# A mixture-of-experts layer on one Trainium2 core: from tile 32 on the shift rows stand eight tiles behind the rows in SyncE's list, and the padding stores go between later tiles

## The chip, the cores and the metric

The kernel runs on one core of one Trainium2 chip. Its time is the device time of one execution in microseconds; the time before is the median of three runs. Engines are named as the profile names them: PE is TensorE (matrix products, with PEld its weight loads), DVE is VectorE, ACT is ScalarE, POOL is GpSimd, SP is SyncE. SP computes nothing here: it works down a list of waits and DMA issues.

## The reference, cut to what matters

The input x is 16 sequences of 512 tokens with 128 features. A scan layer comes first; then every token goes to the best two of eight experts, each a pair of matrix products with a normalisation behind each.

```python
h = _layernorm(x, axis=-1) * (1 + ca) + sa
x = x + ga * _L0_attn_ref(h, ...)
h = _layernorm(x, axis=-1) * (1 + cb) + sb
x = x + gb * _L0_ffn_ref(h, ...)
...
def _L0_ffn_ref(x, Wr, br, W1, b1, g1, be1, W2, b2, g2, be2):
    logits = xt @ Wr + br
    p = jax.nn.softmax(logits, axis=-1)
    probs, idx = jax.lax.top_k(p, K)
    ...
    h = jnp.einsum('td,edf->etf', xt, W1) + b1[:, None, :]
    h = _layernorm(jax.nn.relu(h), g1, be1)
    y = jnp.einsum('etf,efd->etd', h, W2) + b2[:, None, :]
    y = _layernorm(jax.nn.relu(y), g2, be2)
    gate = (jax.nn.one_hot(idx, E, dtype=x.dtype) * probs[..., None]).sum(axis=1)
    out = jnp.einsum('te,etd->td', gate, y)
```

## The kernel before, in words

**Two phases.** In the first (`mixer_step`, to about 160 us) the 16 sequences pass the scan layer; the second normalisation gives rows h, and each token's row is written twice, once for each of its experts, into the DRAM tensor `expert_rows`, which has one region for each expert. POOL does that with indirect DMAs (`store_rows`, L703). In the second phase (`expert_step`, 160 to about 475 us) 135 tiles of 128 rows are worked off in order, tile i with the weights of one expert. A table in on-chip memory says for each tile from which row it starts and which expert it has.

**One tile.** The number behind each engine is the step in which it works on tile i; step s is the one in which PE computes the hidden layer of tile s.
- SP loads the tile's 128 rows into one of eight buffers `hrow` (`load_rows`, L549).
- PE turns them (`turn_rows`, L1650, step i-2), ACT and DVE split them into a high and a low part (L820, L1224).
- PE computes the hidden layer (L1667 to L1669, step i), ACT takes the relu (L824), DVE the statistics (L1229), PE turns it (L1675, step i+2), ACT copies it back (L828).
- PE multiplies it with the second weights (`values`, L1685, step i+4).
- DVE scales and shifts that product (v0, L1452, step i+5). For this it needs the first third of the tile's *shift row*: three vectors of 128 numbers of the expert, the same for all 128 partitions, which SP loads with one DMA of 192 KB (`load_shifts`, L570).
- ACT relu (L948), DVE statistics and vg (L1463, second third of the shift row, step i+7). The last third is added to give the result y: either by DVE itself (`direct`, L1444, odd tiles below 44 and the last five) or by ACT (L956) and POOL (`add_shift`, L719).
- DVE works out in step i, from the rows, where each result row goes (target, L1435); POOL stores y with an indirect DMA into `expert_results` (`store_results`, L731).

PE's four-tile beat: before every fourth tile PE also puts the first biases of four tiles into its banks (`biases`, L1659), so every fourth tile is longer.

**What sets SP's order.** SP's list is written out by hand. For each tile index i, `load_next(i)` (L571) issues: on every fourth i the table entries and the biases of four tiles (L528, L535, L561); then, after waiting until tile i-8 has been turned (`t3_done`) and its targets are computed (`target_ready`), the rows of tile i; then the shift row of tile i-6 (`SHIFT_LAG` is `SLOTS - 2`, 6). The shift row's buffer is free when the result y of the tile that used it last is done, so `load_shifts(j)` waits for that y. Buffers are shared as `ring` says: up to tile 31 there are sixteen, from tile 32 on eight. So the shift row of tile 40 is the first that waits for a tile only eight before it: for the y of tile 32.

```python
user = last_user(i)
if user is not None and direct(user):
    sp.wait_ge(direct_y_ready, direct_count(user))
elif user is not None:
    sp.wait_ge(y_ready, shifted_count(user))
```

**What else SP issues between tiles.** `store_padding(e)` (L596) writes 128 rows of padding behind the last row of expert e's region, one store for each of eight experts; on e = 0 and e = 4 it first loads four counts (L593). It must be done before the rows of tile 73 are loaded. `load_gb` (L627) comes after tiles 30, 32, 34 and 36. `load_early(b)` (L616, 512 KB) loads results of batch b for the output, after tile index 54 for b = 0, 61 for b = 1 and so on to 131; for b = 0 it waits in `results_of` (L609) until the results of tiles 31 to 38 have landed in DRAM. `store_early(b)` (L620) stores finished output.

Of the kernel before, what the change touches and what calls it, by code (L numbers as in the profile page):

```python
# [6 lines left out]
def adaln_ssm_moe_kernel(nc, x_in, win_in, bin_in, bp_in, cp_in, dp_in, wout_in, bout_in, wr_in, br_in,  # L7
# [27 lines left out]
    DI, NS = bp_in.shape  # L35
    CI = DI // P
    E, _, F = w1_in.shape
    CF = F // P
    TOPK = 2
# [3 lines left out]
    EXPERT_TILES = TOPK * NT + E - 1  # L43
# [9 lines left out]
    ROUND1 = (ROUND1_BATCHES * J * TOPK * P - E * (P - 1)) // P  # L53
# [14 lines left out]
    with ExitStack() as ctx:  # L68
# [13 lines left out]
        SLOTS = 8  # L82
# [166 lines left out]
        def direct(i):  # L249
            return i >= LAST_SHIFTED or i % 2 == 1 and i < ROWS_UNTIL  # L250

        def direct_count(i):
            return sum(direct(n) for n in range(i + 1))

        def shifted_count(i):
            return i + 1 - direct_count(i)
# [5 lines left out]
        def piece_tile(b, j):  # L262

            return FIRST_COMBINED + (b * J + j) * (LAST_PIECE - FIRST_COMBINED) // (EARLY * J - 1)
# [14 lines left out]
        def ring(i):  # L279

            return i % (2 * SLOTS) if i < WIDE_UNTIL else i % SLOTS
# [5 lines left out]
        def shift_lane(i):  # L287

            return ring(i) // 2 if i < WIDE_UNTIL else ring(i)
# [6 lines left out]
        def last_user(i):  # L296

            return max((m for m in range(i) if ring(m) == ring(i)), default=None)
# [148 lines left out]
        def tiles(b):  # L447

            return bass.ds(b * J, J)
# [3 lines left out]
        def _(sp):  # L453
# [72 lines left out]
            def load_row_numbers(i):  # L526
                ids = range(i, min(i + AT_ONCE, EXPERT_TILES))
                _, values = nc.values_load_multi_w_load_instructions(  # L528
                    tile_row[0:1, i:ids[-1] + 1], engines=(mybir.EngineType.SP,), min_val=0, max_val=SPARE + (NSPARE - 1) * P,
                    skip_runtime_bounds_check_because="cut off at the first and the last row where the table is written")  # L530
                row_of.update(zip(ids, values))
# [10 lines left out]
            def rows_of_batches(count):  # L542
                for m in range(ROW_LANES):
                    sp.wait_ge(rows_stored[m], row_groups(count, m))
# [3 lines left out]
            def load_rows(i, n):  # L548
                sp.dma_start(hrow[n], rows_d[bass.ds(row_of[i], P), :]).then_inc(hrow_loaded[n], 16)  # L549

            SHIFT_LAG = SLOTS - 2

            def load_b1(i):
                load_expert_numbers(i)
                if i == 0:
                    sp.wait_ge(b1_stored, 32)
                if i >= 2 * TOGETHER:
                    sp.wait_ge(h_done, i - 2 * TOGETHER + 1)
                for n in together(i):
                    part, turn = b1_rows(n)  # L560
                    sp.dma_start(b1_ring[part, turn, :].bitcast(F32), b1_d[bass.ds(expert_of[n], 1), :, :].rearrange("o k f -> (o k) f")  # L561
                                 ).then_inc(b1_loaded[turn], 16)

            def load_shifts(i):
# [5 lines that stand above are left out]
                sp.dma_start(shift_rows[ring(i)], shifts_d[bass.ds(expert_of[i], 1), :].broadcast_to([P, 3 * D])).then_inc(shifts_loaded[shift_lane(i)], 16)  # L570

            def load_next(i):
                if i % AT_ONCE == 0:
                    load_row_numbers(i)
                    load_b1(i)
                sp.wait_ge(t3_done, i + 1 - SLOTS)
                sp.wait_ge(target_ready, i + 1 - SLOTS)
                load_rows(i, i % SLOTS)
                load_shifts(i - SHIFT_LAG)

            for n in range(SLOTS):
                load_rows(n, n)
            for n in range(0, SLOTS, TOGETHER):
                load_b1(n)
            for n in range(SLOTS - SHIFT_LAG):
                load_shifts(n)
            count_of = {}

            def store_padding(e):
                if e == 0:  # L590
                    sp.wait_ge(counts_ready, 1)
                if e % AT_ONCE == 0:
                    _, values = nc.values_load_multi_w_load_instructions(  # L593
                        cnt_i[0:1, GROUPS - 1, e:e + AT_ONCE], engines=(mybir.EngineType.SP,), min_val=0, max_val=T)
                    count_of.update(zip(range(e, e + AT_ONCE), values))
                sp.dma_start(rows_d[bass.ds(count_of[e] + e * REGION, P), :], padding[:]).then_inc(padding_stored, 16)  # L596

            PADDED_AT = ROUND1 - E
            for i in range(SLOTS, ROUND1):
                load_next(i)  # L600
                if i >= PADDED_AT:
                    store_padding(i - PADDED_AT)
            FIRST_BATCHES = GROUP_ENDS[2]
            LAST_ROWS = FIRST_BATCHES * J * TOPK - E + 1
            sp.wait_ge(table_ready, 2)
# [5 lines left out]
            def load_early(b):  # L611
                if b == 0 or tiles_for(b) > tiles_for(b - 1):
                    results_of(tiles_for(b))
                if b >= 2:
                    sp.wait_ge(early_sum_ready, (b - 1) * J)
                sp.dma_start(early01[b % 2], results_v[:, tiles(b), :]).then_inc(early_loaded[b % 2], 16)  # L616

            def store_early(b):
                sp.wait_ge(early_out_ready, (b + 1) * J)
                sp.dma_start(out_v[:, tiles(b), :], X[:, tiles(b), :]).then_inc(out_stored, 16)  # L620

            def load_gb(n):
                part = slice(n * B // GB_PARTS, (n + 1) * B // GB_PARTS)
                if n == 0:
                    sp.wait_ge(gb_stored, 16)
                    sp.wait_ge(w2_ready, W2_STEPS)
                sp.dma_start(gb_rows[:, part, :], gates_d.rearrange("o (b d) -> o b d", b=B)[:, part, :].broadcast_to(  # L627
                    [P, B // GB_PARTS, D])).then_inc(gb_loaded, 16)

            GB_AT = {ROUND1 + 6 + 2 * n: n for n in range(GB_PARTS)}  # L630
            STORED_AT = {piece_tile(b, 0) + 23: b for b in range(EARLY - 2)}
            LOADED_AT = {piece_tile(b, 0) + 1: b for b in range(EARLY)}
            for i in range(ROUND1, EXPERT_TILES):
                if i == LAST_ROWS:
                    sp.wait_ge(padding_stored, 16 * (NSPARE + E))
                    rows_of_batches(B)
                load_next(i)
                if i in GB_AT:
                    load_gb(GB_AT[i])
                if i in LOADED_AT:  # L640
                    load_early(LOADED_AT[i])
                if i in STORED_AT:
                    store_early(STORED_AT[i])
# [4 lines left out]
            def load_late(b):  # L648
                results_of(tiles_for(b))
                sp.dma_start(late01[b], results_v[:, tiles(b), :]).then_inc(late_loaded[b], 16)  # L650

            sp.wait_ge(early_sum_ready, (EARLY - 1) * J)
            load_late(11)
            for n in range(EXPERT_TILES - SHIFT_LAG, EXPERT_TILES):
                load_shifts(n)
# [936 lines left out]
        def _(pe):  # L1592
# [48 lines left out]
            def load_expert(i):  # L1641
                _, values = nc.values_load_multi_w_load_instructions(
                    experts[0:1, i:i + 1], engines=(mybir.EngineType.PE,), min_val=0, max_val=E - 1,
                    skip_runtime_bounds_check_because="a count of experts, cut off at E - 1")
                expert_of[i] = values[0]
# [234 lines left out]
```

## Time and profile before

| | |
|---|---|
| time, median of 3 runs | 499.58 us (499.39 to 500.2) |
| the profiled execution | 501.55 us, its span 499.8 us |
| PE busy | 480.2 us, 96% of the span |
| DVE busy | 447.7 us, 90% |
| ACT busy | 406.4 us, 81% |
| POOL busy | 349.4 us, 70% |
| granted TensorE clock | 0.998 of full speed |
| DMA, queue of SP's issues | 71860 packets, 60.48 MB, 48.6% of 16 engines' span |

The span runs from the first to the last instruction that the profiler recorded; the time of the execution has 1.75 us more. A row of the timeline has the start in us from the span's start, the duration, engine, line, operation, what it writes and reads, how many instructions are merged in it, and in brackets the idle time of the engine before it with what ended it. Tiles have no number in the profile: they are counted, the last hidden layer (L1667), row load and shift load being tile 134's. An SP row is the issue of a DMA, not its transfer.

### The profile page before, as it was taken

What the parts mean: (1) busy time and instruction counts of PE and PEld (TensorE: products, weight loads), DVE (VectorE), ACT (ScalarE), POOL (GpSimd) and SP (SyncE); (2) the same over time, 40 slices, a digit from 0 to 9 for tenths busy, and PEclk for the clock granted to TensorE, in tenths of its full rate; (3) what the DMA queues carried; (4) which work ended last, traced back from release to release, by engine and by line L of the source; (5) the groups of instructions that cost most, each with busy time, mean ns of one, the idle gap of its engine ahead of it and who ended that gap; (6) DMA issues with size and microseconds to landing.
All of it is one profiled execution on the core that took longest, in us unless ns stands there. A gap on an engine that the chain in (4) does not pass through costs nothing. (4 is left out here: it accounts for less than half of the span.)

```text
span 499.8 us, 15142 instructions
## 1 busy us (share of the span) xinstructions
PE 480.2 (96%) x3151; PEld 373.4 (75%) x3151; DVE 447.7 (90%) x2210; ACT 406.4 (81%) x1118; POOL 349.4 (70%) x461
## 2 busy tenths in 40 slices
PE   7999999999998899999999999999999999999994
PEld 6456666565676788888878888888788888888861
DVE  6878999989897999899998999999899999999994
ACT  3678899988856778787876898989889888989883
POOL 1003676766777777888888778888786888888871
PEclk9999999999999999999999999999999999999999
DMA  6990511124111889877539787577577667567655
GB/s 164 312 260 23 132 51 49 55 70 102 54 49 57 186 168 162 205 233 200 134 93 178 196 199 200 136 207 205 160 192 191 173 184 213 159 177 209 191 176 168
DMA packets 80365, 78.37 MB, mean 157 GB/s; under 512 B 11434, under 2 KB 73053, under 8 KB 80277
## 3 DMA queue, kind: packets, MB, share of 16 engines
q1 hardware_dynamic: 71860, 60.48, 48.6%
q0 software_dynamic: 8416, 16.93, 9.6%
q8 instruction: 30, 0.49, 0.4%
q14 instruction: 59, 0.48, 0.3%
HBM read 55.20 MB, written 22.62 MB: 156 GB/s over the span
## 5 line engine op out<-in xcount | busy, mean ns | idle before, releaser
L703 POOL DMA_INDIRECT expert_rows<-rows_ring,slot x128 | 123.9, 968 | 87.2 <-issue 68.5
L731 POOL DMA_INDIRECT expert_results<-y,target x119 | 120.5, 1012 | 33.2 <-issue 28.8
L1685 PE MATMUL bank<-W,h2T 128*128 x720 | 97.0, 278 | 2.1 <-issue 0.9
L1685 PEld LDWEIGHTS bank<-W,h2T 128*128 128x128 f32 x720 | 87.5, 191 | 14.0 <-issue 7.5
L948 ACT ACTIVATE v<-wmod 128x128 f32<-128x128 f32 x135 | 41.7, 309 | 31.8 <-DVE vg L1463 28.5
L1667 PE MATMUL bank<-W1hi,h3hi 128*128 x135 | 65.4, 485 | 1.5 <-DVE h3lo L1224 1.5
L1229 DVE BATCH_NORM_STATS2 stf<-h1T 128x6 f32<-128x512 f32 x90 | 59.3, 660 | 0.0
L813 ACT ACTIVATE n<-X,nm,rs 128x128 f32<-128x128 f32 x128 | 52.6, 488 | 7.2 <-DVE nm L1392 7.1
L1452 DVE SCALAR_TENSOR_TENSOR wmod<-bank,rse,shifts 128x128 f32<-128x128 f32 x119 | 40.9, 344 | 15.9 <-PE bank L1685 14.4
L960 ACT ACTIVATE sde<-mve,eps 128x2 f32<-128x2 f32 (+1 forms) x138 | 40.7, 295 | 17.8 <-DVE mve L1476 15.6
L1675 PE MATMUL bank<-ident_wr,h1T 128*128 128x128 f32 x360 | 54.5, 274 | 0.1
L828 ACT ACTIVATE h2T<-bank 128x512 f32<-128x512 f32 x90 | 52.8, 587 | 1.3 <-PE bank L1675 1.3
L1668 PE MATMUL bank<-W1lo,h3hi 128*128 x135 | 53.3, 395 | 0.0
L1669 PE MATMUL bank<-W1hi,h3lo 128*128 x135 | 53.3, 395 | 0.0
L824 ACT ACTIVATE h1T<-bank 128x512 f32<-128x512 f32 x90 | 53.0, 589 | 0.0
L1685 PE MATMUL bank<-W,third_rT 128*128 x360 | 48.3, 277 | 1.5 <-DVE wmod L1452 0.9
L1685 PEld LDWEIGHTS bank<-W,third_rT 128*128 128x128 f32 x360 | 43.6, 191 | 6.8 <-issue 3.4
L1463 DVE SCALAR_TENSOR_TENSOR vg<-v,mve,shifts 128x128 f32<-128x128 f32 x119 | 44.1, 370 | 0.0
L1675 PEld LDWEIGHTS bank<-ident_wr,h1T 128*128 128x128 f32 x360 | 41.4, 141 | 1.5 <-issue 0.3
L1224 DVE TENSOR_TENSOR h3lo<-bank,h3hi 128x128 fp32r<-128x128 f32 x135 | 38.0, 282 | 1.5 <-ACT h3hi L820 1.4
L1471 DVE BATCH_NORM_STATS2 sty<-v 128x6 f32<-128x128 f32 x135 | 38.1, 282 | 0.2
L1650 PE MATMUL bank<-ident_wr,hrow 128*128 128x128 f32 x135 | 36.3, 273 | 0.6 <-DMA hrow<-expert_rows 0.6
(260 smaller groups left out, 1187.0 us busy)
## 6 DMA issues: line engine op xcount, KB each, us to landing
shifts<-expert_shifts SPq DMA_DIRECT2D x119, 192.0 KB
hrow<-expert_rows SPq DMA_DIRECT2D x135, 65.0 KB
xi<-expert_results SPq DMA_DIRECT2D x12, 512.0 KB, 5.5
out_x<-X SPq DMA_DIRECT2D x15, 256.0 KB
X<-in_L_attn_x SPq DMA_DIRECT2D x7, 512.0 KB, 7.4
b_ring<-b_two_parts SPq DMA_DIRECT2D x135, 4.0 KB
W1lo<-in_L_ffn_W SPq DMA_DIRECT2D x4, 512.0 KB, 6.2
expert_rows<-rows_ring,slot POOLq DMA_INDIRECT x128
```

What stands on the lines that cost most here:

```text
L703: nc.gpsimd.indirect_dma_start(out=rows_d, out_offset=bass.IndirectOffsetOnAxis(ap=slot[q][:, n // TOPK, n % TOPK:n % TOPK + 1], axis=0), ...
L731: nc.gpsimd.indirect_dma_start(out=results_d, out_offset=bass.IndirectOffsetOnAxis(ap=target[i % TARGETS][:], axis=0), in_=y[k], in_offset ...
L813: ins = nc.scalar.activation(dst[:, j:j + 1, :], X[:, bass.ds(b * J + j, 1), :], ACT.Identity, bias=nm_[:, x_tiles + j:x_tiles + j + 1], s ...
L824: nc.scalar.activation(r[i % DEPTH], hidden_bank(i)[:], ACT.Relu).then_inc(r_ready, 1)
L828: nc.scalar.activation(rT[i % DEPTH], turned_bank[:], ACT.Copy).then_inc(rT_ready, 1)
L1229: vec.bn_stats(stf[i % 2][:], r[i % DEPTH]).then_inc(stf_ready, 1)
L1463: vec.scalar_tensor_tensor(wide(vg[p][:]), wide(v[p][:]), mve[p][:, 1, 0:1], wide(shift_rows[ring(s - 7)][:, D:2 * D]), ALU.subtract, ALU. ...
L1667: mm(h, h3hi[i % DEPTH], W1hi[:, bass.ds(e, 1), :], start=False, stop=False)
L1668: mm(h, h3hi[i % DEPTH], W1lo[:, bass.ds(e, 1), :], start=False, stop=False)
L1669: mm(h, h3lo[i % DEPTH], W1hi[:, bass.ds(e, 1), :], start=False, stop=True).then_inc(h_done, 1)
L1675: ins = tr(turned_bank[:, ch * P:(ch + 1) * P], r[i % DEPTH][:, ch * P:(ch + 1) * P], ident[:])
L1685: ins = mm(acc, rT[i % DEPTH][:, ch * P:(ch + 1) * P], W2[:, bass.ds(e * CF + ch, 1), :], start=(ch == 0), stop=(ch == CF - 1))
```

## The change

Up to index 31 nothing changes in `load_next`. At 32 and 33 no shift row is issued, and from 34 on the shift row of tile i-8 follows the rows of tile i. The two shift rows that are then left over (127 and 128) are issued after the loop, before the wait that precedes `load_late(11)`. The padding stores leave indices 16 to 23 and stand at 38, 42, 46, 50, 54, 58, 62 and 66; the two loads of counts go with them, to 38 and 54. The same instructions are issued as before, 972 rows in SP's list in both; the other engines' lists are the same.

```diff
-            SHIFT_LAG = SLOTS - 2
+            SHIFT_LAG, LATE_SHIFT_LAG, LATE_FROM = SLOTS - 2, SLOTS, 32
...
                 load_rows(i, i % SLOTS)
-                load_shifts(i - SHIFT_LAG)
+                if i < LATE_FROM:
+                    load_shifts(i - SHIFT_LAG)
+                elif i >= LATE_FROM + LATE_SHIFT_LAG - SHIFT_LAG:
+                    load_shifts(i - LATE_SHIFT_LAG)
...
-            PADDED_AT = ROUND1 - E
             for i in range(SLOTS, ROUND1):
                 load_next(i)
-                if i >= PADDED_AT:
-                    store_padding(i - PADDED_AT)
...
+            PADDED_AT = {ROUND1 + 14 + 4 * e: e for e in range(E)}
+            assert max(PADDED_AT) < LAST_ROWS
...
                 load_next(i)
+                if i in PADDED_AT:
+                    store_padding(PADDED_AT[i])
                 if i in GB_AT:
                     load_gb(GB_AT[i])
...
+            for n in range(EXPERT_TILES - LATE_SHIFT_LAG, EXPERT_TILES - SHIFT_LAG):
+                load_shifts(n)
             sp.wait_ge(early_sum_ready, (EARLY - 1) * J)
             load_late(11)
```

SP's list before, at indices 32 and 33 (`hrow_0` and `hrow_1` are the rows of tiles 32 and 33; the shift rows behind them are those of tiles 26 and 27):

```order
L549 ISA [waits target_ready,t3_done]
L549 DMA hrow_0<-expert_rows 128x130
L570 ISA [waits y_ready]
L570 DMA mixT_both<-expert_shifts 128x384
L627 DMA gb_rows<-gate_b_rows 128x512
L549 ISA [waits target_ready,t3_done]
L549 DMA hrow_1<-expert_rows 128x130
L570 ISA [waits direct_y_ready]
L570 DMA mixT_both<-expert_shifts 128x384
```

SP's list now, at indices 32 to 34 (the shift row at the end is tile 26's):

```order
L549 ISA [waits target_ready,t3_done]
L549 DMA hrow_0<-expert_rows 128x130
L627 DMA gb_rows<-gate_b_rows 128x512
L549 ISA [waits target_ready,t3_done]
L549 DMA hrow_1<-expert_rows 128x130
L549 ISA [waits target_ready,t3_done]
L549 DMA hrow_2<-expert_rows 128x130
L570 ISA [waits y_ready]
L570 DMA mixT_both<-expert_shifts 128x384
```

The shift row of tile 26 stood behind the rows of tile 32 and stands behind those of tile 34. From here on each row load has two shift loads fewer ahead of it.

SP's list before, at index 54 and the rows of 55 (`hrow_6` and `hrow_7`; `xi_0<-expert_results` is `load_early(0)`, the shift rows are those of tiles 48 and 49):

```order
L549 DMA hrow_6<-expert_rows 128x130
L570 ISA [waits y_ready]
L570 DMA shifts<-expert_shifts 128x384
L616 DMA xi_0<-expert_results 128x4x256 [waits result_stored3,result_stored4,result_stored2,result_stored5,result_stored1,result_stored6,result_stored0,result_stored7]
L549 ISA [waits target_ready,t3_done]
L549 DMA hrow_7<-expert_rows 128x130
L570 ISA [waits direct_y_ready]
L570 DMA shifts<-expert_shifts 128x384
```

SP's list now, at the same place (the shift rows are those of tiles 46 and 47):

```order
L549 DMA hrow_6<-expert_rows 128x130
L570 ISA [waits y_ready]
L570 DMA shifts<-expert_shifts 128x384
L596 TENSOR_LOAD cnt_i
L596 ISA x8
L599 ISA
L599 DMA expert_rows<-padding 128x130
L616 DMA xi_0<-expert_results 128x4x256 [waits result_stored3,result_stored4,result_stored2,result_stored5,result_stored1,result_stored6,result_stored0,result_stored7]
L549 ISA [waits target_ready,t3_done]
L549 DMA hrow_7<-expert_rows 128x130
L570 ISA [waits direct_y_ready]
L570 DMA shifts<-expert_shifts 128x384
```

The load of counts and a padding store have come in ahead of the wait for results, and the shift rows of tiles 47 and 48, which stood ahead of that wait, stand behind it.

## Rows read from the trace of the kernel before

**Rows 1.** The page, part 1: busy us, share of the span, instructions

```profile
PE 480.2 (96%) x3151; PEld 373.4 (75%) x3151; DVE 447.7 (90%) x2210; ACT 406.4 (81%) x1118; POOL 349.4 (70%) x461
```

**Rows 2.** Timeline of PE: hidden layers (L1667) and turned rows (L1650)

```profile
209.69 0.50 PE L1667 MATMUL bank<-W1hi,h3hi 128*128 x1
...
256.27 0.51 PE L1667 MATMUL bank<-W1hi,h3hi 128*128 x1
...
258.44 0.48 PE L1667 MATMUL bank<-W1hi,h3hi 128*128 x1
...
261.08 0.48 PE L1667 MATMUL bank<-W1hi,h3hi 128*128 x1
...
264.27 0.48 PE L1667 MATMUL bank<-W1hi,h3hi 128*128 x1
...
281.89 0.48 PE L1667 MATMUL bank<-W1hi,h3hi 128*128 x1
...
286.78 0.50 PE L1667 MATMUL bank<-W1hi,h3hi 128*128 x1
...
295.98 0.50 PE L1667 MATMUL bank<-W1hi,h3hi 128*128 x1
...
342.99 0.51 PE L1667 MATMUL bank<-W1hi,h3hi 128*128 x1
...
350.71 0.33 PE L1650 MATMUL bank<-ident_wr,hrow 128*128 128x128 f32 x1 [0.30 <-DMA hrow<-expert_rows]
...
353.24 0.50 PE L1667 MATMUL bank<-W1hi,h3hi 128*128 x1
```

**Rows 3.** Waits of PEld, whole span: us in total, times, longest

```profile
PEld bank L1650 <- DMA hrow<-expert_rows: 1.7, 3, 0.8
```

**Rows 4.** Waits of SP's queue, whole span: us in total, times, longest

```profile
SPq L570 <- POOL y L719: 46.6, 36, 10.1
```

**Rows 5.** Timeline of SP, 244 to 260 us: issues of rows (L549) and shift rows (L570)

```profile
244.32 0.33 SPq L549 DMA_DIRECT2D hrow<-expert_rows  x1
254.91 0.34 SPq L570 DMA_DIRECT2D shifts<-expert_shifts  x1
255.81 0.33 SPq L549 DMA_DIRECT2D hrow<-expert_rows  x1
...
259.53 0.36 SPq L549 DMA_DIRECT2D hrow<-expert_rows  x1
```

**Rows 6.** Timeline of SP: the rows of tile 85

```profile
344.42 0.34 SPq L549 DMA_DIRECT2D hrow<-expert_rows  x1
```

**Rows 7.** Timeline of POOL: y of tile 38 and the store of its result

```profile
266.85 0.48 POOL L719 TENSOR_TENSOR y<-vs,shifts 128x128 f32<-128x128 f32 x1
...
268.79 0.97 POOL L731 DMA_INDIRECT expert_results<-y,target  x1 [0.30 <-issue]
```

**Rows 8.** Timeline of SP: a shift row, then counts and the first padding store

```profile
177.05 0.36 SPq L570 DMA_DIRECT2D mixT_both<-expert_shifts  x1
179.21 0.37 SPq L596 DMA_DIRECT2D expert_rows<-padding  x1
```

**Rows 9.** Timeline of SP: `load_early(0)` and the shift rows of tiles 49 and 50

```profile
274.52 0.39 SPq L616 DMA_DIRECT2D xi<-expert_results  x1
...
275.70 1.05 SPq L570 DMA_DIRECT2D shifts<-expert_shifts  x1
...
280.13 0.36 SPq L570 DMA_DIRECT2D shifts<-expert_shifts  x1
```

**Rows 10.** Busy time by stretch: PE, PEld, DVE, ACT, POOL, PEclk, DMA share, GB/s

```profile
264.00:275.00 11.00, 10.70 (x76) 8.91 (x75) 9.43 (x41) 7.56 (x23) 8.80 (x11) 1.00 0.98 176
```

**Rows 11.** Line 616 (`load_early`), all eleven

```profile
DMA to landing us min/median/max: 5.2/5.4/7.0
```

**Rows 12.** Timeline of DVE: v0 of tile 18 and of tile 40

```profile
206.98 0.35 DVE L1452 SCALAR_TENSOR_TENSOR wmod<-bank,rse,shifts 128x128 f32<-128x128 f32 x1 [0.46 <-issue]
...
258.37 0.35 DVE L1452 SCALAR_TENSOR_TENSOR wmod<-bank,rse,shifts 128x128 f32<-128x128 f32 x1 [0.32 <-DMA shifts<-expert_shifts]
```

## The prediction

> **What bounds the kernel now.** The page's busy times come first: PE is busy 96% of the span, DVE 90% [rows 1]. So a gain can only be time in which PE stands still or waits, and it shows best as a beat. In PE's timeline the hidden layers of four tiles in a row take 295.98 - 286.78 = 9.20 us where nothing disturbs them: three tiles of 2.15 and a fourth, with the biases, of 2.75 [rows 2]. I went through the expert phase with this ruler. Between the hidden layers of tile 44 (256.27) and tile 56 (286.78) twelve tiles take 30.5 us; three beats would be 27.6, so 2.9 us are lost. Between tiles 80 and 84 (342.99 to 353.24) 10.25 us pass: 1.05 lost [rows 2].
>
> Next, who ended the waits. PE's weight loads for turning rows waited three times for `hrow`, 1.7 us in all [rows 3], and one of PE's own such waits is tile 85's, at 350.71 [rows 2]; its rows had been issued at 344.42, right behind an early load [rows 6]. The other place is tile 47. SP issued the rows of tile 46 at 244.32 and then nothing until the shift row of tile 40 at 254.91: its longest wait is for POOL's y, 10.1 us [rows 4, 5]. That is y of tile 32, the first that gates a shift row only eight tiles later. Behind it stood the rows of tile 47 (255.81) and 48 (259.53) [rows 5], and the beats of tiles 46 and 47 are 2.64 (258.44 to 261.08) and 3.19 (to 264.27) in place of 2.15 [rows 2]. So rows came late although their buffers had long been free.
>
> **Part 1: two shift rows fewer ahead of each row load.** After the change the rows of tiles 47 and 48 stand ahead of the shift row of tile 40 and no longer wait for y of tile 32. They are issued once tiles 39 and 40 have their targets. Tile 46's rows, which wait for those of tile 38, went at 244.32 [rows 5], so these come a beat or two later, before 249: some 7 to 9 us gained. Later, where SP is held by y, each row load comes two tiles, 4.6 us, earlier. Stalls for rows should go everywhere: at most 2.9 us between tiles 44 and 56 and 1.05 at tile 84, together 3.95.
>
> The shift rows themselves: their issue waits for y of eight tiles before, in either order. Where y is the last thing to come, they are issued at the same moment as before. Tile 40's, issued at 254.91, was used at 258.37 after DVE had waited 0.32 us for it [rows 5, 12], 3.46 us from issue to use. PE needs that value only when it multiplies tile 41, so it cost PE nothing there. I cost this half at nothing, except where something other than y holds SP. Such a place exists.
>
> **Part 2: the place that takes it back.** After index 54 SP waits for the results of tiles 31 to 38 before it issues `load_early(0)`. Before, the shift rows of tiles 47 and 48 stood ahead of that wait; now they stand behind it. POOL ends y of tile 38 at 266.85 + 0.48 = 267.33 and issues that tile's result at 268.79 [rows 7]. POOL runs without pause from one 4.2 us pair of tiles to the next there, so I take these times as unchanged however fast PE gets. Then:
> - The shift row of tile 46 waits for that y: issued at 267.4.
> - The counts and the padding store behind it: 179.21 - 177.05 = 2.16 us from a shift row's issue to the padding's, and 0.37 more [rows 8]. SP reaches the wait at 270.0.
> - The last result must have landed. Before, SP came free for `load_early(0)` at 274.52 [rows 9], 5.7 us after POOL's issue, with the DMA engines at 0.98 in that stretch, full of shift and row loads that SP had sent out in a burst [rows 10]. The two bounds for the issue of `load_early(0)` are thus 270.0 (no wait at all) and 274.5. I take the middle, 272.2: the burst is gone, but a padding store and a shift row still share the engines with the result.
> - The shift row of tile 47 follows 275.70 - 274.52 = 1.18 us later [rows 9] and lands hardly before the early load ahead of it, which takes 5.2 at the least [rows 11]: 277.4.
> - The shift row of tile 48 has the biases of four tiles ahead of it: before, the second shift row stood 280.13 - 274.52 = 5.61 us behind the early load, of which 0.7 was an issue of 1.05 us where 0.33 is usual [rows 9, 5]. So 277.1, and with tile 40's 3.46 it can be used at 280.6.
> - From a late v0 to the next hidden layer: v0 of tile 18 started late at 206.98 and the hidden layer of tile 24 at 209.69, 2.7 us later [rows 12, 2]; that is a fourth tile, so 2.7 - 0.6 = 2.1 for another. Hidden layer of tile 54: 280.6 + 2.1 = 282.7. Before it was 281.89 [rows 2].
>
> So PE, which by then is 2.9 us ahead, is held until it is 0.8 us behind the kernel before. From there both run at the beat.
>
> **A rule weighed.** The result's 64 KB took 5.7 us from issue to release of SP, including the time in which POOL generates its descriptors [rows 7, 9]. The Trainium skill, in DMA: Bandwidth & Descriptors (Anatomy of one DMA, SWDGE path), fits such a DMA with about 2.0 us plus bytes over 436 GB/s, 2.15 us here as an estimate; the trace disagrees where the engines are full. By it SP would be free at 271, and the sum would be about -1.5 in place of the -0.25 below.
>
> **Part 3: the padding stores.** Eight stores and two loads of counts leave indices 16 to 23. SP comes earlier to the shift rows behind them, and the 0.5 us that tile 24 lost to a late one [rows 12, 2] may go. I cost that at nothing: PE is caught by the hold of part 2, whose time POOL sets. At the new places each store costs SP about 0.5 us in which it would wait for y anyway; only index 54 has its price above.
>
> **The sum.** +0.8 (hold at tile 54, from which the 2.9 is already taken off) - 1.05 (tile 84) = -0.25 us. The profiled execution took 501.55 us, of which 499.8 are the span; it would become 501.3. The median of the runs, 499.58, lies 0.4% under it; with the same difference it becomes 499.3. Bounds: with 270.0 the hold is 2.2 shorter, -2.45 in all, 497.1; with 274.5 it is 2.3 longer, +2.05, 501.6.
>
> **The rivals.**
> - *The rows' stalls go and no hold takes their place.* For it: DVE's waits for shift rows were small. Against it: the order of SP's list at index 54 is certain. It would give 499.58 - 3.95 = 495.6. Chance 0.12.
> - *A short hold.* The results land as fast as the fitted rule has it, or have landed when SP comes: `load_early(0)` between 270.0 and 271.2, -2.45 to -1.25, 497.1 to 498.3, say 497.6. For it: SP no longer fills the engines just then. Chance 0.15.
> - *A long hold, slower than before.* The mechanism is one: the wait for the results of tile 38, with the shift rows of tiles 47 and 48 behind it. If the result takes its old 5.7 us, `load_early(0)` goes at 274.5, shift row 48 is used at 282.9, hidden layer 54 comes at 285.0, 3.1 later than before, less 1.05: 501.6. It decides against the change from the point at which the early load is issued later than 272.5. The Trainium skill speaks for it in the same page (Issuing engines are not separate DMA queues): DMAs of all issuing engines share 16 engines and interleave, so POOL's store waits with SP's loads. Chance 0.23.
> - *The change doesn't do what it says:* row loads are held by something else, `target_ready` or the biases, and the gaps stay: 499.6. Against it: by the beat, tile 39's targets are there before 249, not at 255. Chance 0.05.
>
> **How the numbers follow.** The forecast, rows' stalls gone and given back by a hold of middle length, has 0.45 and the time 499.3, with its own range from 498.3 to 500.3. About 0.2%, 1.0 us, is what a measurement of this kernel can tell from no change. Faster by more: 0.12 + 0.15 + 0.09 of the forecast's lower end = 0.36. Slower: 0.23 and 0.02 of the rest = 0.25. Within: 0.39. The range leaves out the full gain (0.12) and a little beyond the long hold: 496.8 to 501.7.
>
> **What the profile of the changed kernel would show.** Right: SP's gap between 245 and 254 begins after the rows of tile 48; PE's timeline has no wait on `hrow` in the expert phase, and the 1.7 us of PEld are near 0; beats of 2.15 and 2.75 from tile 44 to 52; then one gap of DVE before v0 of tile 47, put down to the shift rows' DMA, of 2 to 3 us at about 277, PE waiting on DVE's v0 behind it; `load_early(0)` issued between 271 and 274; and tile 84 in beat. The sum is wrong if hidden layer 54 is not at 282.7 within 1 us: earlier, and a short hold or none is true; later, and the long one is. If the hidden layers of tiles 46 and 47 still lose time, the rows were not the cause. If a new stall comes after tile 60, behind later early loads, I have overlooked that shift rows there have as little room as at tile 47.

## The result, and the profile after: 0.34% slower

| | before | after |
|---|---|---|
| median of 15 runs each | 499.65 us (499.15 to 500.88) | 501.35 us (500.01 to 503.25) |
| ratio, 95% interval | | 1.0034 (1.0023 to 1.0046) |
| the profiled execution, its span | 501.55, 499.8 us | 502.17, 500.4 us |
| a second profiled execution (other runs of the same two kernels) | 499.14, 497.3 us | 500.19, 498.4 us |

The forecast was 499.3 us, no change as the likeliest case. The time is inside the range of 496.8 to 501.7 and on the side that had 0.25. The second execution of before lies 0.5 us under its median and the first 1.9 above it; which of them is read turned out to matter.

The busy times say nothing new: PE 481.1 us, DVE 447.5, POOL 348.2 [rows 1]. SP's waits do, over the whole span (us in total, times, longest; L577 waits for targets, ahead of the rows):

```profile
SPq L577 <- DVE target L1441: 38.9, 36, 8.7
...
SPq L570 <- POOL y L725: 18.8, 13, 3.4
```

The wait for y was 46.6 us in 36 times, 10.1 the longest [rows 4]; now SP comes to a shift row later, and it is the next row load that waits, for targets. The wait on `hrow` that PE's weight loads had [rows 3] has no row any more, and no row load comes late. The first half of the change does what it says. SP's timeline around index 54 [rows 5, 9]:

```profile
251.04 0.36 SPq L549 DMA_DIRECT2D hrow<-expert_rows  x1
254.91 0.36 SPq L570 DMA_DIRECT2D shifts<-expert_shifts  x1
...
267.59 0.34 SPq L570 DMA_DIRECT2D shifts<-expert_shifts  x1
269.70 0.36 SPq L599 DMA_DIRECT2D expert_rows<-padding  x1
272.75 0.39 SPq L616 DMA_DIRECT2D xi<-expert_results  x1
273.38 1.04 SPq L549 DMA_DIRECT2D hrow<-expert_rows  x1
274.62 0.34 SPq L570 DMA_DIRECT2D shifts<-expert_shifts  x1
275.82 1.57 SPq L561 DMA_DIRECT2D b_ring<-b_two_parts  x4
277.62 0.36 SPq L549 DMA_DIRECT2D hrow<-expert_rows  x1
278.16 0.36 SPq L570 DMA_DIRECT2D shifts<-expert_shifts  x1
```

The rows of tile 48 go at 251.04, ahead of the shift row of tile 40 at 254.91. The shift row of tile 46 is the one at 267.59; tile 47's has to wait behind the early load until 274.62, tile 48's until 278.16. The results that SP waits for are those of tiles 37 and 38, stored by POOL [rows 7]:

```profile
266.93 0.47 POOL L725 TENSOR_TENSOR y<-vs,shifts 128x128 f32<-128x128 f32 x1
...
268.86 0.97 POOL L737 DMA_INDIRECT expert_results<-y,target  x1 [0.30 <-DVE target L1441]
```

DVE's v0 of tiles 47 and 48, and what it waited for:

```profile
278.60 0.35 DVE L1458 SCALAR_TENSOR_TENSOR wmod<-bank,rse,shifts 128x128 f32<-128x128 f32 x1 [2.86 <-issue]
...
281.91 0.35 DVE L1458 SCALAR_TENSOR_TENSOR wmod<-bank,rse,shifts 128x128 f32<-128x128 f32 x1 [1.76 <-DMA shifts<-expert_shifts]
```

The gap of tile 47 is put down to "issue", nothing that the profile shows; but v0 starts 3.98 us after the issue of its shift row, and the next one, 3.75 us after its own, names the DMA. PE's timeline: hidden layers (L1673) of tiles 44, 52, 53, 54, 56, 80 and 84, and the `values` (L1691) that stood still between two of them [rows 2]:

```profile
257.04 0.50 PE L1673 MATMUL bank<-W1hi,h3hi 128*128 x1
...
275.80 0.50 PE L1673 MATMUL bank<-W1hi,h3hi 128*128 x1
...
279.21 1.32 PE L1691 MATMUL bank<-W,h2T 128*128 x8 [2.33 <-DVE wmod L1458]
...
281.03 0.78 PE L1673 MATMUL bank<-W1hi,h3hi 128*128 x1
...
284.30 0.48 PE L1673 MATMUL bank<-W1hi,h3hi 128*128 x1
...
289.19 0.50 PE L1673 MATMUL bank<-W1hi,h3hi 128*128 x1
...
345.01 0.50 PE L1673 MATMUL bank<-W1hi,h3hi 128*128 x1
...
354.36 0.50 PE L1673 MATMUL bank<-W1hi,h3hi 128*128 x1
```

Up to tile 52 PE is close to its beat (eight tiles in 18.76 us; two beats are 18.4). Tile 53 then comes 5.23 us after tile 52 in place of 2.15, and tile 54 3.27 after that. From tile 80 to 84 it is 9.35: the stall of tile 84 is gone. One ruler for all kernels below is the time from hidden layer 44 to 56 (beat: 27.6 us) and from 80 to 84 (9.2).

### The profile page after: what moved, and what is told of

It is laid out like the page before. It is cut to its first block and busy times, and to the rows that moved or that the text cites. A ratio compares the mean times of both kernels' runs of the same rounds, so it can differ in the third digit from the quotient of the medians.

```text
span 500.4 us, 15142 instructions
## 1 busy us (share of the span) xinstructions
PE 481.1 (96%) x3151; PEld 376.3 (75%) x3151; DVE 447.5 (89%) x2210; ACT 405.4 (81%) x1118; POOL 348.2 (70%) x461
## 5 line engine op out<-in xcount | busy, mean ns | idle before, releaser
L1691 PE MATMUL bank<-W,h2T 128*128 x720 | 98.1, 280 | 3.5 <-DVE wmod L1458 2.9
L1691 PEld LDWEIGHTS bank<-W,h2T 128*128 128x128 f32 x720 | 88.9, 194 | 15.1 <-issue 8.3
L1673 PE MATMUL bank<-W1hi,h3hi 128*128 x135 | 65.7, 487 | 1.4 <-DVE h3lo L1230 1.4
L1691 PE MATMUL bank<-W,third_rT 128*128 x360 | 48.0, 276 | 0.9 <-DVE wmod L1458 0.7
L1691 PEld LDWEIGHTS bank<-W,third_rT 128*128 128x128 f32 x360 | 43.7, 192 | 5.8 <-issue 2.1
```

The lines of the kernel that those rows point to most:

```text
L1673: mm(h, h3hi[i % DEPTH], W1hi[:, bass.ds(e, 1), :], start=False, stop=False)
L1691: ins = mm(acc, rT[i % DEPTH][:, ch * P:(ch + 1) * P], W2[:, bass.ds(e * CF + ch, 1), :], start=(ch == 0), stop=(ch == CF - 1))
```

## The experiments

The theory: the rows' stalls go; SP's wait for results at index 54, with two shift rows behind it, gives more back (A, where an expectation uses letters). Rivals: the padding stores at their new places cost the time (B); the shift rows have too little lead everywhere, not only behind this wait (C); or the loss is the lowered TensorE clock that follows PE's idle time (D). One more point was open beside them: whether before's own stalls, read from one execution, are as large as they looked.

| kernel | median (runs) | ratio to before, 95% | 44 to 56 | 80 to 84 |
|---|---|---|---|---|
| before, two executions | | | 30.51, 29.81 | 10.25, 9.64 |
| after, two executions | 501.35 (15) | 1.0034 (1.0023, 1.0046) | 32.15, 31.82 | 9.35, 9.18 |
| lag_only | 501.62 (8) | 1.0035 (1.0022, 1.0049) | 30.57 | 9.18 |
| padding_only | 500.37 (12) | 1.0008 (0.9996, 1.0020) | 30.97 | 9.87 |
| early0_two_later | 500.24 (12) | 1.0012 (0.9997, 1.0026) | 30.20 | 9.35 |
| lag8_only_32_to_53 | 500.11 (11) | 1.0005 (0.9993, 1.0017) | 30.38 | 9.93 |
| after_filled | 501.83 (10) | 1.0048 (1.0033, 1.0064) | 32.78 | 9.36 |
| combined_from_57 | 498.51 (11) | 0.9969 (0.9958, 0.9981) | 29.82 | 9.23 |
| combined_from_57_again | 498.36 (12) | 0.9980 (0.9967, 0.9993) | 28.37 | 9.25 |
| from_57_only | 499.53 (12) | 0.9989 (0.9970, 1.0008) | 29.67 | 9.31 |
| from_57_lag_only | 497.58 (6) | 0.9956 (0.9943, 0.9969) | 27.98 | 9.30 |
| from_57_lag_again | 497.86 (12) | 0.9968 (0.9953, 0.9982) | 28.02 | 9.30 |

The two rulers are of the profiled execution, one per kernel, and where that one is the fastest of its kernel (lag_only: 499.96) they flatter it. How far: combined_from_57 and combined_from_57_again are the same kernel, one profiled in its slowest execution (499.71) and one in its fastest (497.53), and 44 to 56 takes 29.82 and 28.37 us.

**Lag alone**, the padding back at indices 16 to 23.

```diff
-            PADDED_AT = {ROUND1 + 14 + 4 * e: e for e in range(E)}
+            PADDED_AT = ROUND1 - E
```

> The shift rows stand eight tiles behind from tile 32 on, the padding stores stay at their old places (indices 16 to 23). Theory A (the shift rows of tiles 47 and 48 now stand behind SP's wait for the results of tile 38, and the loss comes from that hold and the clock's fall in it): the hold stays, DVE waits 2 to 3 us before v0 of tile 47, PE waits about 2 us behind it, the clock falls at about 280 us; time 500.6 to 501.4, slower than before. Rival B (the padding stores among later tiles cost it): no slower than before, 499.0 to 499.8, since their cost is gone and the rows are early.

Measured 501.62 us, 1.0035: the whole loss of the change. Its profiled execution has the same picture: v0 of tile 47 and of tile 48 after gaps of DVE, PE waiting behind each and no row late. It shows the kind of the stall and not its size: it is the fastest execution of its kernel, 1.7 us under the median, and its 30.57 us from 44 to 56 are no more than before's 30.51. SP's timeline (the shift rows of tiles 46 and 47, between them the early load, here L619), and DVE's:

```profile
267.17 0.33 SPq L570 DMA_DIRECT2D shifts<-expert_shifts  x1
271.25 0.39 SPq L619 DMA_DIRECT2D xi<-expert_results  x1
...
272.42 1.28 SPq L570 DMA_DIRECT2D shifts<-expert_shifts  x1
```

```profile
277.21 0.35 DVE L1457 SCALAR_TENSOR_TENSOR wmod<-bank,rse,shifts 128x128 f32<-128x128 f32 x1 [1.96 <-issue]
...
280.19 0.35 DVE L1457 SCALAR_TENSOR_TENSOR wmod<-bank,rse,shifts 128x128 f32<-128x128 f32 x1 [1.43 <-DMA shifts<-expert_shifts]
```

With no counts and padding in the way the early load goes 1.5 us earlier than in after, but the shift row behind it takes 4.79 us from issue to use in place of 3.98; the issue alone is 1.28 us of it in place of 0.34. The padding falls as the main cause.

**Padding alone.**

```diff
-            SHIFT_LAG, LATE_SHIFT_LAG, LATE_FROM = SLOTS - 2, SLOTS, 32
+            SHIFT_LAG = SLOTS - 2
```

> The shift rows stay six tiles behind, the padding stores go to every fourth tile from 38 on. Theory A: before's stalls for rows at tiles 46 to 49 stay, a padding store adds its 0.5 us of SP ahead of the rows of tile 47; no long hold at 278; time within 0.6 us of before, 499.6 to 500.3. Rival B: most of the change's +1.7 us shows here, 501.0 or more.

500.37 us, 1.0008 with 1 inside the interval: at most 0.2% in the company of the lag of six. PE's weight loads still wait for the rows of tiles 48, 57 and 85, so it doesn't remove before's stalls.

**Before and after once more**, a second profiled execution of each.

> The kernel before once more, for a second trace. Theory A: the same waits for rows at tiles 47 and 48 behind SP's long wait for y of tile 32, hidden layer of tile 54 at 281 to 282.5; span between 497.5 and 500. If the stalls at tiles 46 to 49 are missing here, the rows' part of my sum rested on one execution.

> The changed kernel once more, for a second trace. Theory A: no wait for rows, a gap of DVE of 2 to 3.5 us before v0 of tile 47 and over 1 us before that of tile 48; the early load issued between 271 and 274.5; hidden layer of tile 54 at 282.5 to 285. If the gap is absent or under 1 us here, the hold can't be what makes the medians differ.

Hidden layers of tiles 44, 56, 80 and 84, before:

```profile
256.42 0.50 PE L1667 MATMUL bank<-W1hi,h3hi 128*128 x1
...
286.23 0.51 PE L1667 MATMUL bank<-W1hi,h3hi 128*128 x1
...
341.85 0.50 PE L1667 MATMUL bank<-W1hi,h3hi 128*128 x1
...
351.49 0.50 PE L1667 MATMUL bank<-W1hi,h3hi 128*128 x1
```

The same of after:

```profile
256.32 0.50 PE L1673 MATMUL bank<-W1hi,h3hi 128*128 x1
...
288.14 0.50 PE L1673 MATMUL bank<-W1hi,h3hi 128*128 x1
...
343.86 0.50 PE L1673 MATMUL bank<-W1hi,h3hi 128*128 x1
...
353.04 0.50 PE L1673 MATMUL bank<-W1hi,h3hi 128*128 x1
```

These two start level (0.1 us apart at tile 44), and after then lies behind by 1.91 us at tile 56, 2.01 at tile 80 and 1.55 at tile 84; the spans differ by 1.1, the medians by 1.7. So the open point is answered: before's stalls cost 2.2 us between 44 and 56 and 0.44 at tile 84 in this execution, not 2.9 and 1.05.

**The early load two indices later.**

```diff
-            LOADED_AT = {piece_tile(b, 0) + 1: b for b in range(EARLY)}
+            LOADED_AT = {piece_tile(b, 0) + (1 if b else 3): b for b in range(EARLY)}
```

> The changed kernel with the first early load (and its wait for the results of tiles 31 to 38) after index 56 in place of 54, so that the shift rows of tiles 47 and 48 stand ahead of that wait again. Theory A: rows stay early, no wait for rows, DVE's gap before v0 of tile 47 goes from 2.9 us to under 0.5, the clock stays at 1.00 there, the hidden layer of tile 54 comes at 279.5 to 281 in place of 284.3; time 496.3 to 497.8, faster than before. Rival C (the shift rows have too little lead everywhere, or DMA traffic is what costs): the gap moves on by two tiles and the time stays near 501.

500.24 us: 1.1 better than after, but not the gain that was expected, and hidden layer 54 comes at 281.51. The shift row of tile 47 is now in time, and tile 48's is the late one, behind counts, padding and the biases of index 56:

```profile
267.07 0.33 SPq L570 DMA_DIRECT2D shifts<-expert_shifts  x1
269.17 0.36 SPq L599 DMA_DIRECT2D expert_rows<-padding  x1
...
270.30 0.61 SPq L570 DMA_DIRECT2D shifts<-expert_shifts  x1
271.84 1.57 SPq L561 DMA_DIRECT2D b_ring<-b_two_parts  x4
...
274.19 0.64 SPq L570 DMA_DIRECT2D shifts<-expert_shifts  x1
```
```profile
279.42 0.35 DVE L1458 SCALAR_TENSOR_TENSOR wmod<-bank,rse,shifts 128x128 f32<-128x128 f32 x1 [2.44 <-DMA shifts<-expert_shifts]
```

From the shift row of tile 46 to that of tile 48, 7.1 us pass without any early load between them. The hold moved by one tile: it is not one wait alone but all that stands between two shift rows. This shift row then takes 5.23 us from issue to use, where after's took 3.75; the early load now goes right behind it (275.13) and may have its part in that, which no run separates. The picture is nearer to C than the theory had it.

**Lag of eight up to index 53 only.** At index 54 (`LATE_UNTIL`) the shift rows of tiles 46, 47 and 48 are issued together, then the lag is six again.

```diff
+                elif i == LATE_UNTIL:
+                    for n in range(i - LATE_SHIFT_LAG, i - SHIFT_LAG + 1):
+                        load_shifts(n)
```

> The changed kernel, but at index 54 the shift rows of tiles 46, 47 and 48 are issued together ahead of the padding store, the wait for results and the early load, and from 55 on they stand six tiles behind again. Theory A: rows of tiles 46 to 54 are early, the shift rows of tiles 47 and 48 are no longer behind the hold, the biases or the early load; PE loses under 1 us between tiles 44 and 56 (hidden layer 56 at 284.5 to 285.8 in place of 289.2); later rows have their old short lead, so 0.4 to 1.0 us at tile 84 come back; time 498.3 to 499.3. Rival B (padding stores among these tiles cost it): 500.5 or more, as they are all still there.

500.11 us, the time of before. The waits of DVE for tiles 47 and 48 are gone, but the rows of tiles 55, 57 and 85 come late again: SP issues the shift row of tile 48 at 271.40, once y of tile 40 is there, and only then the early load (274.17) and the rows of tile 55 (274.81). PE's wait for these:

```profile
279.20 0.33 PE L1657 MATMUL bank<-ident_wr,hrow 128*128 128x128 f32 x1 [0.73 <-DMA hrow<-expert_rows]
```

What the shift rows gave back, the rows took.

**PE kept busy in the gap** (18 extra products of 128x128 at step 52, whose results nothing reads).

```diff
+                if s == 52:
+                    pe.wait_ge(rT_ready, s - 2)
+                    for _ in range(18):
+                        mm(turned_bank[:, 0:P], ident[:], ident[:], start=True, stop=True)
```

> The changed kernel with 18 products of 128 columns on PE (about 2 us) put ahead of the second-layer products of tile 48, where PE otherwise stands idle 2.3 us; their result is overwritten and part of no output. Theory D (the fall of the granted clock to 0.5 at 280 us follows from this idle time and is part of the loss): the clock stays at 1.00 between 278 and 290, the hidden layers of tiles 53 and 54 follow v0 of tiles 47 and 48 by 2.1 us in place of 2.4, time 0.2 to 0.5 us under the changed kernel's. Rival E (the clock falls for another reason): the fall is still there at about 280.

The clock's fall went away and the time did not come down: 501.83 us. A stretch of after and of the filled kernel (columns as in [rows 10]):

```profile
280.00:284.00 4.00, 4.00 (x21) 3.55 (x20) 2.12 (x10) 2.26 (x8) 1.61 (x3) 0.57 0.96 175
```

```profile
280.00:284.00 4.00, 4.00 (x34) 3.77 (x34) 2.46 (x12) 1.86 (x7) 1.25 (x2) 1.00 0.72 185
```

But this run doesn't price the clock, for the filling was longer than the gap. PE's filling (L1821) and the product behind it, and DVE's v0 of tile 48:

```profile
276.26 4.18 PE L1821 MATMUL bank<-ident_wr 128*128 128x128 f32 x36
...
280.28 1.06 PE L1691 MATMUL bank<-W,h2T 128*128 x8
```

```profile
281.37 0.35 DVE L1458 SCALAR_TENSOR_TENSOR wmod<-bank,rse,shifts 128x128 f32<-128x128 f32 x1 [2.77 <-PE bank L1691]
```

v0 of tile 47 was done at 277.41, PE's product for tile 48 began only at 280.28, and DVE waited for that product and not for the shift row. The price can be read from other rows. In after v0 of tile 48 waited for its shift row while PE's product was there, so up to that moment the lower clock cost nothing. From it to hidden layer 54 it took 2.39 us (281.91 to 284.30), in the second execution 2.32 (280.94 to 283.26), and 2.09 in lag_only, early0_two_later and combined_from_57, where the clock stayed at 1.00. So the clock's fall follows from the gap, and it is worth 0.2 to 0.3 us of the 2.4 that tile 54 lies behind before. And lag_only's median loses as much, though its trace has no fall at that place.

**The early combination from tile 57 on.** If the theory is right, a wait for results that lie four tiles further back costs nothing.

```diff
-        FIRST_COMBINED, LAST_PIECE = 53, EXPERT_TILES + 1
+        FIRST_COMBINED, LAST_PIECE = 57, EXPERT_TILES + 1
```

> The changed kernel with the whole of the early combination begun four tiles later (first piece at tile 57 in place of 53), so that the first early load stands after index 58. Theory A (a hold in SP's list where the early load, its wait for results and the biases of four tiles come together while the shift rows have no lead): by index 58 the results of tile 38 have long landed, SP is not held, and the shift rows of tiles 47 to 50 go at y's pace ahead of the early load; DVE's gaps before v0 of tiles 47 and 48 are under 0.5 us, hidden layer of tile 54 at 279.5 to 280.8; time 497.8 to 499.0. Rival C (shift rows with too little lead anywhere in this stretch): the gap appears at tile 50 or 51, as large as before, and the time is 500 or more.

498.51 us, 0.31% faster than before. The time was as expected, the gap was not: DVE no longer waited for the shift row of tile 47, but still 1.87 us for that of tile 48, and 1.17 us for that of tile 44, with no early load near: signs for C, beside the hold.

```profile
278.68 0.35 DVE L1458 SCALAR_TENSOR_TENSOR wmod<-bank,rse,shifts 128x128 f32<-128x128 f32 x1 [1.87 <-DMA shifts<-expert_shifts]
```

Three more kernels split this gain: the same once more, the edit on the kernel before, and the edit with the lag of eight and the padding left where it was.

> The same kernel as the earlier run with the combination begun four tiles later, on the same chip as the two above: 498.5, 1.4 us below the kernel before (ratio 0.997), 498.0 to 499.0; the ratio above 0.999 would mean that the first measurement was chance.

> The kernel before, with the early combination begun four tiles later (first early load after index 58 in place of 54) and nothing else. Two readings of the gain of 0.31% over the kernel before that the same edit gave on top of the whole change. Reading 1: the gain is the rows' stalls that the lag of eight takes away, once the hold at index 54 no longer gives them back. Then the edit alone leaves the stalls of rows 47, 54 and 55 (1.3 + 0.4 + 0.5 us in the second trace of before) and saves little, since in the kernel before the early load cost at most the 0.5 us of tile 84 and of 54: 499.0 to 500.0 beside 499.9, ratio 0.998 to 1.001. Reading 2: the gain is the early combination itself being later, the lag has no part in it: 498.3 to 498.8, ratio 0.9965 to 0.998.

> Lag of eight and the early combination four tiles later, with the padding stores left at indices 16 to 23. It tells what the moved padding is worth once the hold is gone. The padding's move alone gave +0.4 us (interval across zero) with the lag of six. If its move costs SP time at indices 38 to 66, this version is 0.2 to 0.5 us below the one with the padding moved: 498.0 to 498.4. If it is worth nothing, the same as that: 498.3 to 498.8.

On one chip: 498.36, 499.53 and 497.58, the last 0.4 us under its expected range. The later combination alone is not clear of zero (0.9970 to 1.0008) and PE's wait for rows is still there:

```profile
PEld bank L1650 <- DMA hrow<-expert_rows: 1.3, 2, 0.7
```

If the lag and the later combination did not work on each other, 1.0035 and 0.9989 would make 1.0024; together they measured 0.9956. So the gain needs the lag of eight and the place without a hold together. SP's list with the padding moved (combined_from_57_again), from the shift row of tile 42 to that of tile 48:

```profile
258.80 0.33 SPq L570 DMA_DIRECT2D shifts<-expert_shifts  x1
259.33 0.35 SPq L599 DMA_DIRECT2D expert_rows<-padding  x1
...
267.31 0.33 SPq L570 DMA_DIRECT2D shifts<-expert_shifts  x1
269.41 0.35 SPq L599 DMA_DIRECT2D expert_rows<-padding  x1
...
274.25 0.71 SPq L570 DMA_DIRECT2D shifts<-expert_shifts  x1
```

and with the padding left (from_57_lag_only):

```profile
258.48 0.33 SPq L570 DMA_DIRECT2D shifts<-expert_shifts  x1
...
266.95 0.33 SPq L570 DMA_DIRECT2D shifts<-expert_shifts  x1
...
271.77 0.36 SPq L570 DMA_DIRECT2D shifts<-expert_shifts  x1
```

The L570 rows are the shift rows of tiles 42, 46 and 48. They are 0.3, 0.4 and 2.5 us later with the padding: tile 46's waits for y in both, and then shift row to padding store at index 54, with the counts between, takes 2.10 us (267.31 to 269.41) that nothing covers. With the padding left, 44 to 56 takes 27.98 us, 0.4 over the beat.

> The same kernel as the run with the lag of eight, the combination four tiles later and the padding left at indices 16 to 23, a second time, on another chip or at another time, since its first median rests on six runs. If the gain is real: 497.3 to 498.3 and a ratio of 0.9945 to 0.997; hidden layer 44 to hidden layer 56 within 28.5 us and no row late. If the first run was lucky: a ratio of 0.998 or more, as with the padding moved.

On a further chip 497.86 us, 0.9968 (0.9953 to 0.9982), and 28.02 us. This is the best version found: 0.3 to 0.4% faster than before and, by the ratios, some 0.7% faster than after. Not all that the rulers show arrives: from hidden layer 84 to 134 the kernels with the later combination take 117.0 to 118.6 us, before 117.4 and 116.5; why was not looked into. How much of it the padding's place is worth is not settled: the ratios with it moved (0.9969, 0.9980) and left (0.9956, 0.9968) overlap.

## Why the prediction was wrong

**Part 1, right.** Row 48 at 251.04, not before 249, but ahead of the shift row of tile 40; no waits on `hrow`; beats kept to tile 52; 80 to 84 in beat. "Does nothing" is out.

**Part 2, right in kind, short in size.** Each step of the hold, forecast and measured in after: shift row 46 267.4, 267.59; SP behind the padding 270.0, 270.06; early load 272.2, 272.75; shift row 47 usable 277.4, used at 278.60; shift row 48 issued 277.1, 278.16, and used at 280.6, 281.91; hidden layer 54 282.7, 284.30. In the second execution the last is 283.26. So the hold came 0.6 to 1.6 us later than forecast. Four terms made that: the early load 0.55 later than my middle; the second shift row 5.41 behind the early load, where I had taken 0.7 off for a long issue that came again (1.04 on the rows of tile 55); 3.75 us from issue to use in place of 3.46; and 2.39 from v0 to hidden layer in place of 2.1, which is the lower clock. The result itself took 3.9 us from POOL's issue (268.86) to SP's release (272.75), where it had taken 5.7 before; the DMA engines' share over the two stretches was 0.65 and 0.99, and in lag_only it took 2.8 us at a share of 0.50. By the fit of the Trainium skill (DMA: Bandwidth & Descriptors, Anatomy of one DMA, SWDGE path) it would be an estimated 2.15; the trace does not agree, in either kernel.

**The sum, wrong, in its term +0.8.** The step that failed is "So PE, which by then is 2.9 us ahead, is held until it is 0.8 us behind the kernel before." Hidden layer 54 came 2.4 us behind the kernel before, in both pairs of executions: 284.30 against 281.89, and 283.26 against 280.81. Two sizes were wrong in it. One is the hold, 0.6 to 1.6 us later than forecast, as above. The other is the base. The hold sets a moment; what it costs is the distance to where the kernel before is at that moment, and I took that from one execution, 1.9 us over the kernel's median. In before's second execution hidden layer 54 comes at 280.81, not 281.89, and tile 84 loses 0.44, not 1.05. My own 282.7 against these gives +1.89 - 0.44 = +1.45 us in place of -0.25. The median stands about a fifth of the way from the second execution to the first (0.5 of 2.4 us), so by interpolation the sum is some +1.1, 500.7 us: slower. Against the second execution the base makes 1.1 of the 1.65 us that were missing and the hold 0.56; against the first the hold makes all of it. Which weighs more at the medians stays open. I had written that the execution stood 0.4% above the median, and then used the difference as if the surplus lay elsewhere; 1.3 of the 2.4 us between the two executions lie in the two stalls that I was counting (30.51 - 29.81 and 10.25 - 9.64).

**Part 3, a wrong cover.** "At the new places each store costs SP about 0.5 us in which it would wait for y anyway": with the lag of eight the wait for y has fallen from 46.6 to 18.8 us, and where SP does not wait, nothing hides a store or the counts, as the pair of lists above shows. It cost little in the change only because the hold at index 54 came anyway.

**The rivals.** The long hold is what happened in effect, 501.6 forecast and 501.35 measured, although the early load went at 272.75 and not at 274.5. So that the two numbers lie so close is luck; the direction is not: with the base of before's second execution it decides from an early load at 272.2 - (282.7 - 280.81 - 0.44) = 270.75, not from 272.5. The place was certain, the price was not, and by that base 0.23 was too little.

## What to carry to other kernels

A wait in a queue that is written by hand prices everything behind it: before moving loads backwards in such a list, find the next wait of another kind (here for results in DRAM) and see which of the moved loads end up behind it. When stalls are counted as a gain, read them in more than one execution, or in one near the median; a surplus of 0.4% was as large as the effect, and half of it lay in the stalls. And if a change removes one stall and makes another, look for the second one's own lever before undoing the first: moving the early combination by four tiles turned 0.34% slower into 0.3% faster.

## What was not expected of the hardware

- PE stood still for 2.33 us up to 279.21, and from about 280.1 the granted clock was at half, 1.2 GHz, for 3.4 us (mean 0.57 from 280 to 284); a hidden layer's product took 0.78 us in place of 0.50. In the second execution it was at half from about 278.1, again for 3.4 us, with an idle time of 1.79 us just before. With PE busy through the gap it stayed at 1.00. In lag_only, with idle times of 1.43 and 0.59 us, it stayed too.
- Now and then one DMA issue takes SP 0.8 to 1.3 us, where 0.33 is usual. One stood right behind the early load in after (1.04), in its second execution (0.79), in lag_only (1.28) and in before (1.05 [rows 9]). But it doesn't belong to the early load: others have none near (1.23 us at 260.07 in before, 1.27 at 259.64 in after), and in padding_only the two issues behind the early load took 0.35 and 0.34. In after's second execution three stand at 177.87, 191.14 and 204.37, 13.3 us apart. The cause stays open. A term of this kind recurs; it should not be taken off as an accident.
